# One list of pieces for layer 1: local attention of batch 1 and the MLP of batch 0 placed under the top-16 halves

## The reference

```python
h = _ln(x) * (1 + sc_msa) + sh_msa
h = _self_attn(h, w_qkv, b_qkv, w_so, b_so)          # windows of 64 tokens, shifted by 32
x = x + h * g_msa
h = _ln(x) * (1 + sc_mca) + sh_mca
h = _topk_cross_attn(h, context, w_q, b_q, w_kv, b_kv, w_co, b_co)
    # scores (b,h,q,77); top_s, top_i = lax.top_k(scores, 16); softmax over the 16; weighted sum of v
x = x + h * g_mca
h = _ln(x) * (1 + sc_mlp) + sh_mlp
u = h @ w_m1 + b_m1                                   # 1024 wide: a, b
x = x + (silu(a) * b @ w_m2 + b_m2) * g_mlp
```

## Time and profile before

| what | us |
|---|---|
| median of three timed runs | 459.71 |
| the profiled execution's own time | 461.02 |
| its span, first to last instruction | 459.3 |
| PE busy | 366.4 |
| DVE busy | 303.5 |
| ACT busy | 204.1 |
| POOL busy | 109.4 |

### The profile page before, as it was taken

How to read it: one execution, slowest core, us unless ns; L and a number is a source line. 1 busy time by engine, 2 the same in 40 slices (tenths; PEclk the granted TensorE clock), 3 DMA queues, 4 the chain that set the end, 5 groups by cost and what they waited for, 6 DMA issues and landing times.

```text
span 459.3 us, 8983 instructions
## 1 busy us (share of the span) xinstructions
PE 366.4 (80%) x3326; PEld 214.9 (47%) x3326; DVE 303.5 (66%) x1281; ACT 204.1 (44%) x304; POOL 109.4 (24%) x130
## 2 busy tenths in 40 slices
PE   0958899999989987899979798866585566675885
PEld 0746322323333155677646547643363344453454
DVE  4386976999897056667236544236979999995332
ACT  1141036666656935566532032433444455654411
POOL 8047200002510011001022400011443544443010
PEclk9977658999999998999989586977877777776989
DMA  7236031112000000000000000000000000000000
GB/s 211 59 112 185 24 123 53 52 55 87 3 1 2 0 1 1 1 2 1 1 0 2 6 2 6 4 3 1 1 3 0 1 2 1 1 1 1 1 24 24
DMA packets 10811, 12.16 MB, mean 26 GB/s; under 512 B 2378, under 2 KB 9103, under 8 KB 10767
## 3 DMA queue, kind: packets, MB, share of 16 engines
q1 hardware_dynamic: 10469, 11.55, 8.6%
q0 software_dynamic: 256, 0.01, 0.0%
q10 hardware_dynamic: 42, 0.01, 0.0%
HBM read 8.69 MB, written 2.62 MB: 25 GB/s over the span
## 4 chain that ended last, share of the span: by engine, by line
PE 55%; DVE 28%; ACT 8%; issue 5%; POOL 1%; DMA 1%; SPq 1%; ACTq 0%; DVEq 0%
PE psum L1350 6%; PE psum L1410 6%; PE psum L1378 5%; PE psum L1363 5%; DVE mx L1125 4%; DVE left L1180 4%; DVE left L1187 4%; PE psum L1511 4%; PE psum L1251 3%; PE psum L1393 3%; DVE top L1177 3%; PE psum L1421 3%; DVE top L1184 2%; PE psum L1433 2%; PE psum L1448 2%
## 5 line engine op out<-in xcount | busy, mean ns | idle before, releaser
L1125 DVE TENSOR_REDUCE mx<-psum 128x1 f32<-128x512 f32 x128 | 80.2, 680 | 11.2 <-PE psum L1350 11.1
L731 ACT ACTIVATE big<-psum 128x1024 f32<-128x1024 f32 x64 | 62.4, 1022 | 42.3 <-PE psum L1363 42.0
L1350 PE MATMUL psum<-KS,QS 72*128 72x512 bf16 x128 | 51.1, 431 | 5.3 <-DVE mx L1125 4.4
L1410 PE MATMUL psum<-kblk,qf 128*128 128x308 f32 x128 | 48.0, 508 | 1.1 <-DVE qf L1058 0.8
L1421 PE MATMUL psum<-ident,pr 128*77 128x128 f32 x256 | 39.3, 305 | 9.9 <-POOL pr L672 9.8
L561 POOL TENSOR_TENSOR rstd<-vareps,minus_half 128x4 f32<-128x4 f32 x12 | 12.2, 1018 | 143.5 <-DVE vareps L901 143.4
L1421 PEld LDWEIGHTS psum<-ident,pr 128*77 128x77 f32 x256 | 35.3, 171 | 18.1 <-POOL pr L672 13.3
L1363 PE MATMUL psum<-QS,KS 75*128 75x512 bf16 x128 | 40.4, 404 | 0.4
L672 POOL TENSOR_TENSOR pr<-pr,early 128x616 f32<-128x616 f32 x16 | 23.9, 1493 | 56.0 <-ACT early L841 38.8
L1378 PE MATMUL psum<-big,V 128*9 128x512 f32 x256 | 35.2, 623 | 0.5 <-ACT big L731 0.5
L1350 PEld LDWEIGHTS psum<-KS,QS 72*128 72x128 bf16 x128 | 12.0, 103 | 47.4 <-DVE mx L1125 24.6
(11 more groups left out here) (195 smaller groups left out, 663.3 us busy)
## 6 DMA issues: line engine op xcount, KB each, us to landing
QS<-scr_q SPq DMA_DIRECT2D x8, 288.0 KB
KS<-scr_k SPq DMA_DIRECT2D x8, 288.0 KB
scr_q<-qp SPq DMA_DIRECT2D x2, 384.0 KB, 2.7
scr_k<-kp SPq DMA_DIRECT2D x2, 384.0 KB, 3.3
early<-in_L_xcond_w_ada_dram SPq DMA_DIRECT2D x1, 576.0 KB, 7.2
wmlp<-in_L_xcond_W_mlp_dram SPq DMA_DIRECT2D x2, 256.0 KB, 3.2
scr_k<-kp SPq DMA_DIRECT2D x2, 256.0 KB, 3.5
wm<-in_L_xcond_w_m_dram SPq DMA_DIRECT2D x1, 512.0 KB, 4.4
```

Source lines behind the costliest of these rows:

```text
L731: freed(act.activation(pT[:, u % 2, 1024 * half:1024 * (half + 1)], ps, ACT.Exp), "sT", 0, u, half)
L1125: freed(dve.tensor_reduce(mx[:, n % 3, NT * hh + q:NT * hh + q + 1], ps, AX_X, ALU.max), "max", t, q)
L1350: filled(pe.matmul(ps, QS[b][0:ROWS, h, q * P:(q + 1) * P], KS[b][0:ROWS, h, :], start=True, stop=True), "max", j, q)
L1410: last = pe.matmul(ps[:, 512 * a:512 * a + HH // 2 * S], qf[:, b, i * P:(i + 1) * P], kb[:, c0:c0 + HH // 2 * S], start=True, stop=True)
```

## The change

Layer 1 is written as one table, `ORDER`, which all four engines read. An item is a letter with indices; "<" marks an item that only PE (and the room planner) takes at that place, ">" one that only the reading engines take. The letters: a projections of q and k, v, x window maxima, y their transpose, E window scores and exp, F times v, G transpose and division, o p t q the projection chain, s S n N the layer norm and bias, Q cross scores, A B C D the four DVE phases of a half, d the difference and its exp, K the exp of `left` and the product, T V U transposes, product with v and division, m one chunk of the MLP, r its output.

In words:
1. The maxima of b = 1 (x1..) are interleaved with the windows of b = 0 (E, F, G), and its layer norm transposes (t310) stand inside b = 0's maxima.
2. The windows of b = 1 (E4 to E7, F, G) stand under the top-16 halves 1 to 4. The top-16 halves start when b = 0 alone is ready.
3. The MLP of b = 0 (m000 to m003, r00) stands under halves 12 to 15. There Silu is written as u/2 * (1 + tanh(u/2)): ACT does Tanh and Identity (both 0.5 * u), POOL a product and a sum (`swish`), DVE the product with the other half. The MLP of b = 1 keeps Silu.
4. The last tile is split off: after the last half, batch 1's tiles 0 to 2 (part 1) and tile 3 (part 2) go separately through projection, layer norm, MLP and store. The last store's two DMAs are issued by SP and ACT.
5. In both layers the scores contract only the 32 rows that hold the four heads concerned: `kown` (four heads wide) in place of `kblk` (16 wide), two products on different row groups per half. The columns per product (308) stay. `kown` is made once for both layers near the start.
6. `exp_window`, `window_qk` and the like now do one half or one column group per call; `oraw_w` is a buffer of its own for the windows, so is `wqkF`.

Core of the diff:

```diff
+ORDER = """
+    ...
+    K4 V1> Q6 U1< p310< A5 B5 U1> p310> s410 d5 S410 T4 C5 D5 n410
+    ...
+    K11 Q13 A12 B12 m000> d12 T11 m001< C12 D12 V5<
+    ...
+    """
-        kblk = sb("kblk", [P, B, H, S])
+        kown = sb("kown", [P, 2, B, G, S])
-                c0 = S * (HH * (e % 2) + HH // 2 * a)
-                last = pe.matmul(ps[:, 512 * a:512 * a + HH // 2 * S], qf[:, b, i * P:(i + 1) * P],
-                                 kb[:, c0:c0 + HH // 2 * S], start=True, stop=True)
+                r = 2 * (e % 2) + a
+                rows = slice(QUAD * r, QUAD * (r + 1))
+                last = pe.matmul(ps[:, 512 * a:512 * a + G * S], qf[rows, b, i * P:(i + 1) * P], kb[rows, :],
+                                 start=True, stop=True)
+            def swish(b, c):
+                pool.wait_ge(s_half, c + 1)
+                pool.tensor_tensor(sa[b][c % 2], sa[b][c % 2], gT[:, b, c, :], ALU.mult).then_inc(s_swish, 1)
+                pool.wait_ge(s_swish, 2 * c + 1)
+                pool.tensor_tensor(gT[:, b, c, :], sa[b][c % 2], gT[:, b, c, :], ALU.add).then_inc(s_swish, 1)
+            for kind, at in layer1(">"):
+                if kind == "S":
+                    ln_rstd(*at)
+                elif kind == "N":
+                    add_bias(*at)
+                elif kind == "d":
+                    difference(*at)
+                elif kind == "K":
+                    keep_taken(*at)
+                elif kind == "m" and at[0] == 0:
+                    swish(0, at[2])
+            def silu_out(b, p, c):
+                i0, ni = TILES[p]
+                own = slice(i0 * P, (i0 + ni) * P)
+                ps = read_room(act, "m", b, p, c)[:, own]
+                v = VECS["L1_b_m1"] + c
+                if b == 0:
+                    if c >= 2:
+                        act.wait_ge(s_swish, 2 * (c - 1))
+                    act.activation(sa[0][c % 2], ps, ACT.Tanh, scale=0.5, bias=half_b[:, c:c + 1])
+                    act.activation(gT[:, 0, c, :], ps, ACT.Identity, scale=0.5, bias=half_b[:, c:c + 1])\
+                        .then_inc(s_half, 1)
+                else:
+                    if c >= 2:
+                        wait_read(act, "m", b, p, c - 2)
+                    act.activation(sa[b][c % 2][:, own], ps, ACT.Silu, bias=cols[:, v:v + 1]).then_inc(s_silu, 1)
+            def gate_mul(b, p, c):
+                ...
+                if b == 0:
+                    dve.wait_ge(s_swish, 2 * (c + 1))
+                    swished = gT[:, 0, c, :]
+                else:
+                    dve.wait_ge(s_silu, NC_ * (p - 1) + c + 1)
+                    swished = sa[b][c % 2][:, own]
+                freed(dve.scalar_tensor_tensor(out=gT[:, b, c, own], in0=ps, scalar=cols[:, v:v + 1],
+                                               in1=swished, op0=ALU.add, op1=ALU.mult), "m", b, p, c)
```

More of the change, by code:

```diff
@@ L104, in rooms_in_turns @@
     use("M", "mods", 0)
[L105 to L185, removed]
-                if e == at:
-                    use(room, *key)
-            if e > HALVES:
-                for c in (0, 1) if e == HALVES + 1 else (2, 3):
-                    use("X", "mlp", layer, 0, c)
-                    if layer == 1:
-                        use("W", "mlpb", 0, c)
-        use("M", "oT", 2 * layer + 1, 1)
-        use("M", "out", 3 * layer + 1, 1)
-        use("M", "out", 3 * layer + 2, 0)
-        use("M", "lnT", 3 * layer + 2, 1)
-        for c in range(NC_):
-            use("X", "mlp", layer, 1, c)
-            if layer == 1:
-                use("W", "mlpb", 1, c)
-        if layer == 0:
-            use("W", "lnT", 3, 0)
-        use("M", "out", 3 * layer + 2, 1)
@@ L657, in _, with difference @@
                 add_bias(3, b)
-            ctx_blocks(1)
-            ln_rstd(4, 0)
-            add_bias(4, 0)
-            for e in range(HALVES):
+            def difference(e):
                 k = e % 2
@@ new lines, in _ @@
+            ps = read_room(act, "ctxT")
+            freed(act.activation(ctxT[:, :, :], ps[:, 0:2 * B * S].rearrange("p (l n) -> p l n", l=2), ACT.Copy),
+                  "ctxT")
+            for l2 in range(2):
+                ps = read_room(act, "kc", l2)
+                c = VECS["L0_b_kvc" if l2 == 0 else "L1_b_kv"]
+                freed(act.activation(kcT[:, l2, :, :], ps[:, 0:B * S].rearrange("p (b s) -> p b s", b=B),
+                                     ACT.Identity, bias=cols[:, c:c + 1]), "kc", l2)
@@ L883, in _ @@
+            store(act, 1, 2, first=False)
         @block.vector
@@ L1297, in mlp_out @@
                                          gw[n, b][:, c * C:(c + 1) * C], start=(c == 0), stop=(c == NC_ - 1))
-                filled(last, "out", n, b)
+                filled(last, *key)
             pe.wait_ge(s_ident, 1)
@@ new lines, in _ @@
+            for b in range(B):
+                ln_T(0, b)
+            for b in range(B):
+                qk(b)
+            wide_rows(2)
+            for b in range(B):
+                v(0, b)
+            ps = open_room(pe, "ctxT")
+            pe.wait_ge(s_chat, B)
+            for l2, src in enumerate((chat, ctxt)):
+                for b in range(B):
+                    last = pe.transpose(ps[:, (l2 * B + b) * S:(l2 * B + b + 1) * S], src[:, b, :], ident[0:S, 0:S])
+            filled(last, "ctxT")
```

1224 lines of the change are left out of this document (681 added, 543 removed).

## The result

The changed kernel took 469.76 us (median, 465.63 to 472.5) against 459.29 (458.66 to 459.73) before: ratio 1.0227, 95% interval 1.0172 to 1.0283. It is slower; the forecast was 444.5 and faster. The profiled execution of the changed kernel is its fastest one, 465.63 us with a span of 463.6; the span of the kernel before is 459.3.

A forecast was written before the change was run, and what follows sets the result against it. Bounds: PE in layer 0's cross attention, short waits in layer 1 before the halves, DVE in the halves, nothing wide in the tail. −6 − 14.0 + 20.3 − 15.5 = −15.2 us, from 459.71 to 444.5 us, range 438 to 451.

The forecast's parts named there:

- Scores on 32 rows: Layer 0's cross attention: a half's two products run side by side, saving 0.5 us per half; 6 us less taken.
- The drain rule: Rival in layer 0's cross scores: changing tiling mode drains the array, so no gain; 450.5 us, chance 0.06.
- The head: Layer 1 up to the first MAX8: earlier projections, mixed maxima and windows, fewer windows before the first half; 14.0 us less.
- The halves: Layer 1's top-16 halves: more DVE work, waits for swish and late PE products; 123.3 us, 20.3 us more.
- the late products: Top-16 halves: chunk 1's MLP products on PE wait for the room until the first gate product; 1.9 us taken.
- the chain starts anew at every end of a half: Halves 12 to 15: swish chain of 5.3 us restarts after each half; DVE waits 2.5, 4.65, 4.15, 4.65, together 16 us.
- The tail: From the last MATCH_REPLACE8 to the end: 26.4 us against 41.9, 15.5 us less.
- ends 1.4 us late: Tail: batch 0's `mlp_out` on PE (3.81 us), started 8.8 us into half 15, ends 1.4 us after the last MATCH_REPLACE8.
- The start: Start to the third division (`res`) of layer 0's self-attention: forecast change 0.
- The slower rival: Top-16 halves: PE at the low clock becomes their bound, decided below a mean clock of about 0.55; 462.5 us, chance 0.07.

The follow-up runs named there:

- x_extra: The changed kernel plus one unread whole-array product (128 rows, 204 columns) per half in layer 0's cross scores: 466.5 us, ratio 1.0180 to the kernel before.
- x_blocks: The changed kernel with layer 0's cross scores back on the whole array, layer 1's still on 32 rows: 461.8 us, ratio 1.0106 to the kernel before.
- x_rows: The kernel before with only the cross scores of both layers put on 32 rows: 465.3 us, ratio 1.0197 to the kernel before.
- x_loop: The changed kernel, whole-array scores in both layers, GpSimd's swish behind the kept keys, VectorE's product behind the second MAX8: 451.1 us, ratio 0.9848 to before.
- x_dve: The changed kernel, whole-array scores in both layers, swish on VectorE as one operation, Tanh and Identity half a tile earlier: 448.7 us, ratio 0.9807 to before.
- x_moved: The changed kernel with Tanh, Identity and GpSimd's swish half a tile earlier: 464.3 us, ratio 0.9953 to the kernel before.
- x_both: x_moved with layer 0's cross scores also back on the whole array: 458.9 us, ratio 0.9963 to the kernel before.
- x_r00: The changed kernel with batch 0's `mlp_out` behind batch 1's output projection on TensorE, its residual later on VectorE: 467.3 us, ratio 1.0218 to the kernel before.
- x_best: x_dve with the new order of the tail from x_r00: 445.3 us, ratio 0.9683 to the kernel before.

## Why the prediction was wrong, step by step

**Scores on 32 rows, the step that failed.** The prediction took off 6 us for this: "two positions should give nearly 2". The pair gained less: 0.71 us from its start to the next product (x_extra, 191.49 − 190.78) against 1.04, 0.33 us a half and not 0.5. At the low level it took 1.33 (188.13 − 186.80), more than whole-array scores at full clock. Above all, the working held the clock of 1.00 fixed, and the edit itself took it away. x_blocks (+6 us gone), x_rows (+6 us alone) and x_extra (clock back, with more work) show that it is this edit; by what mechanism it lowers the clock is open, as said at x_extra. The term is +6.0 instead of -6, the largest part of the 19.5 us. The drain rule, a rival, would have made it 0: nothing in the rows shows such a pause at full clock, and it does not explain a loss. The low clock was named in the text, but only for the halves.

**The head.** Right, and not by luck: -13.1 for -14.0, and counted from layer 1's first projection batch 1's projections began at 17.6 us (17.6 in the working) and batch 0's transpose at 43.3 (42.7).

**The halves.** The mechanism was right, and was shown by x_loop and x_dve (12 to 13 us back). The waits came to 3.44, 6.16, 4.22 and 4.66 us for 2.5, 4.65, 4.15 and 4.65; POOL's operations took 1.26 (1.24 and 1.27 had been the bounds). The second is longer because of the late products, for which the sum had 1.9 us apart: a pair took 3.54 us, and product with v and next scores behind it kept ACT waiting. Waits and late products together are 18.5 us for 17.9. Of the 4.9 us missing, 3.0 lie in waits of DVE before divisions, two of the windows and one of the cross attention (0.85, 0.92, 1.28 us between 313 and 329 us); the working had set the idle there to nothing. The last 1.3 us were not traced. That the chain starts anew at every end of a half is so in the changed kernel; the ring stands in the order of x_moved and x_both, and it is the expectations of these two that did not see it.

**The tail.** -10.3 for -15.5. The term "ends 1.4 us late" for `mlp_out` was mis-sized: at the low level it took 5.88 and not 3.81 us and started only when ACT had copied the transposes before it, so it ended 4.7 us after the last half (430.90 + 5.88 − 432.07), and DVE waited 4.73 us for the projection behind it. x_r00 gave 3.9 of it back.

**The start.** The 3.5 us less there are probably no effect of the change: over the runs this stretch takes 103.5 to 108.3 us, whatever the edit (x_moved has 108.3, x_rows 104.2), with a granted clock between 0.76 and 0.84 in 30 to 100 us.

**The slower rival** had the low clock in the halves, with PE as their bound; there the clock was 0.70 to 0.72, not 0.55, and DVE waited for POOL. The loss that was not forecast came first of all from another stage. The other timed executions lie 2 to 7 us above the profiled one at clocks of 0.822 to 0.835 against 0.837; in which stage was not seen.

## What to carry to other kernels

Where TensorE is the bound, ask what an edit does to its clock before counting what it saves: here two products on part of the array saved 0.33 us a half at full clock, and with them the clock was at half for 24 us. A wait that returns in every round is a ring: write down who stands behind whom on every engine before moving its start. And work for another batch that is filled into gaps belongs behind the operation on the critical chain, not in front of it: x_r00 took 3.9 us off the tail by that alone.

## What was not expected of the hardware

The granted clock lay at 0.50 for some 24 us while PE was busy all the time (5.00 of 5.00 us from 200 to 205 us). Taking the scores off the whole array brought this in four kernels out of four, and an added product that did no useful work took it away again.

VectorE's swish with both operands in SBUF took 0.68 or 1.91 us for the same 512 columns. In x_dve and x_best, four of the eight took 1.90 to 1.94, each begun about 0.1 us behind POOL's product of kept keys. In x_dve, POOL's product of kept keys ran from 401.46 to 402.94 us, and the slow one began at 401.58:

```profile
401.46 1.48 POOL L735 TENSOR_TENSOR pr<-pr,early 128x616 f32<-128x616 f32 x1 [4.10 <-DVE top L1216]
...
409.85 1.95 POOL L735 TENSOR_TENSOR pr<-pr,early 128x616 f32<-128x616 f32 x1 [5.27 <-DVE top L1216]
```

In the second line DVE was first (409.76, 0.68 us), and POOL's took 1.95. One waits for the other: 1.36 us until POOL ends, and 0.55 for the rest, is the 1.91. The Trainium skill, SBUF — State Buffer, Who interferes with whom, states that a VectorE instruction with two SBUF inputs contends with a GpSimd instruction that reads SBUF, and that the order of issue decides who is blocked; the trace agrees, with 1.91 for 0.68 us one way round and 1.95 for 1.49 the other.
